# Scores of group 0 in a row, four projections moved, and two spreads that wait for rows of maxima

## The chip, the cores and the metric

The kernel runs on one core of a Trainium2 chip. The metric is the device time of one execution in microseconds (us).

## The reference, cut to what matters

Two transformer layers work on 2 batches of 512 tokens of width 256. Each has modulated layer norms, causal attention with 16 heads of 16 dims, and a mixture of experts (top 2 of 8, then top 4 of 16).

```
q, k, v = heads(h @ Wq.T), heads(h @ Wk.T), heads(h @ Wv.T)
scores  = einsum('bhqd,bhkd->bhqk', q, k) / sqrt(16)
attn    = softmax(where(causal, scores, -inf), axis=-1)
x = x + ga * (einsum('bhqk,bhkd->bhqd', attn, v) merged @ Wo.T)
x = x + gb * mixture_of_experts(layernorm(x) * (1 + cb) + sb)
```

## The kernel before, in words

All engines' programs are written out by hand in order, and meet at semaphores. `l` is the layer (0 or 1).

The projections of an attention are 12 *fills*, each one PSUM bank of 128x512: `FILLS` is q, k, q, k, v, v for batch 0 (fills 0 to 5) and v, v, q, k, q, k for batch 1 (fills 6 to 11). PE computes a fill, ScalarE (ACT) moves it out (`move_fill`, two activations for a q or k fill), and VectorE (DVE) splits q and k into three bf16 parts (`split_fill`, three operations). In layer 1 the v fills are moved by DVE inside `split_fill`, with the bias added; in layer 0 `split_fill` of a v fill does nothing.

A pair of q and k fills is a *unit*; unit u holds groups 2u and 2u+1, four heads of one batch each. `spread_unit` copies the parts of a unit into the layout that the score matmuls read: 6 DMAs of 128 KB for q and 6 for k. For units 0 and 1 SP's queue issues the q side and POOL's the k side; for units 2 and 3 POOL issues all 12. Unit 3's spread waits until the by-key scores of groups 0 and 1 are done, because it reuses unit 0's room. In layer 1 POOL issues after it one DMA of 4 MB, a part of layer 1's expert weights, and then runs five elementwise steps.

Attention goes through 8 groups (`NG`). Each is treated twice. First `scores_by_query(g, c)`, 6 pieces (`NA`): PE makes scores, DVE takes row maxima (`maxima(g, c)`) from two double banks in turn, so piece c waits for the maximum of piece c-2. `split_maxima` writes the negated maxima, PE transposes them (`turn_maxima`), DVE copies them to `mT` (`move_maxima`), and SP sends two *rows of maxima* by DMA into the q operand (`send_maxima`, 4 KB, counted in `m_rows[l][g % 2]`). Then `scores_by_key(g, c)`, 10 pieces (`NB`): PE makes scores with the maxima subtracted, ACT takes the exponent (`exponent`), and `weigh_values` and `turn_context` of the group before are worked in between, with `move_context` on ACT and `context` on DVE.

The head of an attention is the by-query scores of groups 0 and 1 mixed with fills 6 to 11. Then follows the loop over p: by-key scores of group p, by-query scores of group p+2 between them. In layer 0, DVE at the end of p = 1 also shapes the modulation rows (`modulation_rows(0)`); SP sends them to DRAM (`keep_rows`) and back over all partitions (`spread_rows`, 1 MB) before it sends the maxima of group 3. Group 3's `send_maxima` is thus queued on SP behind both.

## Time and profile before

| what | value |
|---|---|
| median of 3 runs | 643.21 us (642.0, 643.21, 648.59) |
| profiled execution, its own time | 648.09 us |
| its span from first to last instruction | 646.3 us |
| PE busy, mean granted clock | 508.9 us (79%), 0.882 of full |
| DVE busy | 362.4 us (56%) |
| ACT busy | 241.6 us (37%) |
| POOL busy | 229.3 us (35%) |
| chain that ended last | PE 61%, DVE 16%, DMA 11%, issue 5%, POOL 3%, ACT 3% |

1.8 us of the profiled execution's own time lie outside its span. That execution is 4.9 us above the median of the runs. Attention of layer 0 takes about 15 to 158 us of the span, that of layer 1 about 272 to 425; expert loops take 197 to 247 and 464 to 620.

### The profile page before, as it was taken

Reading aid. Unit: us, or ns where it says so; the run is one execution under the profiler, and the core shown is the slowest. Engines: PE = TensorE matmul, PEld = TensorE weight load, DVE = VectorE, ACT = ScalarE, POOL = GpSimd, SP = SyncE. Lnnn points to the kernel's source line nnn. Section 1 sums busy time; section 2 is a strip of 40 time slices with the busy share of each in tenths; the row PEclk is TensorE's granted clock in tenths of the full one; section 3 lists DMA queues with packets and bytes.
Section 4 is the critical chain, followed back from the end, with each engine's and each line's share of the span. In section 5 each row is a group of like instructions: output and inputs, shape, how many; then the busy total and the mean of one; then the engine's idle time right before and its main releaser. Section 6 shows DMA issues by size and latency. Waiting matters only on the chain.

```text
span 646.3 us, 9621 instructions
## 1 busy us (share of the span) xinstructions
PE 508.9 (79%) x3124; PEld 333.7 (52%) x3124; DVE 362.4 (56%) x831; ACT 241.6 (37%) x530; POOL 229.3 (35%) x233
## 2 busy tenths in 40 slices
PE   3968879997749992266889798744699999999960
PEld 3444545555437892134456365544466666666640
DVE  3529686544652341475877864489654444444425
ACT  1414556652012331030456466423344444444430
POOL 2213023001043424622301700050357777777650
PEclk9979899989567997585989999965799999999995
DMA  8587253163134432268543813460124444444446
GB/s 290 77 101 96 25 116 52 29 255 128 49 122 149 128 102 82 81 86 137 86 53 50 245 68 135 164 264 32 50 51 81 82 78 77 79 78 80 66 47 196
DMA packets 35137, 67.31 MB, mean 104 GB/s; under 512 B 6901, under 2 KB 27845, under 8 KB 34201
## 3 DMA queue, kind: packets, MB, share of 16 engines
q0 software_dynamic: 14496, 31.08, 26.9%
q1 hardware_dynamic: 20312, 35.64, 18.0%
q8 instruction: 27, 0.44, 0.3%
q14 instruction: 14, 0.11, 0.1%
q10 hardware_dynamic: 288, 0.05, 0.0%
HBM read 38.93 MB, written 14.96 MB: 83 GB/s over the span
## 4 chain that ended last, share of the span: by engine, by line
PE 61%; DVE 16%; DMA 11%; issue 5%; POOL 3%; ACT 3%; SPq 1%; POOLq 0%; DVEq 0%; ACTq 0%
PE bank L1619 15%; PE bank L1640 9%; PE bank L1484 5%; PE bank L1454 4%; PE bank L1434 4%; DVE mx L1034 4%; DMA big<-mT 3%; PE bank L1601 2%; PE bank L1372 2%; PE bank L1628 2%; PE bank L1410 2%; PE bank L1616 2%; PE bank L1587 2%; DMA wqkv<-in_wqkv_dram 2%; PE bank L1404 2%
## 5 line engine op out<-in xcount | busy, mean ns | idle before, releaser
L1034 DVE TENSOR_REDUCE mx<-bank 128x4 f32<-128x512 f32 (+2 forms) x96 | 97.9, 1041 | 41.2 <-PE bank L1437 40.7
L755 ACT ACTIVATE ptm<-bank 128x512 f32<-128x512 f32 x160 | 92.4, 597 | 60.9 <-PE bank L1457 58.0
L1619 PE MATMUL bank<-big,ptm 128*128 x280 | 111.5, 522 | 0.0
L629 POOL DMA_INDIRECT ptm<-token_rows,token x70 | 68.9, 984 | 92.8 <-DVE token L1239 47.9
L638 POOL DMA_INDIRECT sums<-ptm,token x47 | 74.4, 1583 | 30.9 <-ACT ptm L832 29.7
L431 POOL DMA_DIRECT2D big<-parts x72 | 38.8, 546 | 122.0 <-DVE parts L960 71.9
L1434 PE MATMUL bank<-big 96*128 96x128 bf16 (+3 forms) x256 | 64.4, 318 | 21.9 <-DMA big<-parts 15.2
L1454 PE MATMUL bank<-big 98*128 98x128 bf16 (+3 forms) x256 | 67.4, 308 | 11.9 <-DMA big<-mT 7.3
L1640 PE MATMUL bank<-big,ptm 128*128 (+1 forms) x280 | 72.6, 382 | 0.0
L1619 PEld LDWEIGHTS bank<-big,ptm 128*128 128x128 f32 x280 | 52.2, 201 | 25.9 <-issue 23.3
L1285 DVE TENSOR_SCALAR tok<-bank 128x256 f32<-128x256 f32 x47 | 20.0, 425 | 79.1 <-PE bank L1619 79.1
L1437 PE MATMUL bank<-constb 128*128 128x128 bf16 x256 | 52.7, 232 | 0.0
L815 ACT ACTIVATE ctxden<-tok 128x256 f32<-128x256 f32 x47 | 19.6, 417 | 86.1 <-DVE tok L1285 86.1
L1640 PEld LDWEIGHTS bank<-big,ptm 128*128 128x128 f32 (+1 forms) x280 | 48.1, 192 | 5.0
L1457 PE MATMUL bank<-constb 128*128 128x128 bf16 x256 | 48.9, 224 | 0.0
L573 POOL TENSOR_TENSOR rstd<-vareps,neghalf 128x4 f32<-128x4 f32 x8 | 8.6, 1071 | 111.0 <-DVE vareps L901 111.0
L1454 PEld LDWEIGHTS bank<-big 98*128 98x128 bf16 x256 | 25.5, 100 | 42.3 <-ACT ptm L755 17.8
L1434 PEld LDWEIGHTS bank<-big 96*128 96x128 bf16 x256 | 26.8, 105 | 38.9 <-issue 28.2
L1357 PE MATMUL bank<-consts,tok 128*128 128x128 f32 x96 | 17.3, 339 | 35.0 <-DVE tok L910 25.9
L1484 PE MATMUL bank<-ptm,big 128*32 128x128 f32 (+3 forms) x512 | 42.1, 448 | 1.4 <-ACT ptm L755 1.4
L1601 PE MATMUL bank<-consts,ptm 128*128 128x128 f32 x140 | 29.0, 291 | 11.7 <-DMA ptm<-token_rows,token 11.7
L1410 PE MATMUL bank<-feat,wqkv 128*128 128x512 f32 x64 | 34.5, 680 | 2.1 <-DMA wqkv<-in_wqkv_dram 1.1
(177 smaller groups left out, 818.9 us busy)
## 6 DMA issues: line engine op xcount, KB each, us to landing
big<-parts POOLq DMA_DIRECT2D x72, 128.0 KB, 5.8
big<-in_moe_dram SPq DMA_DIRECT2D x1, 6144.0 KB, 20.1
big<-in_moe_dram POOLq DMA_DIRECT2D x1, 4096.0 KB, 15.2
big<-in_moe_dram SPq DMA_DIRECT2D x1, 3456.0 KB, 11.2
big<-parts SPq DMA_DIRECT2D x24, 128.0 KB, 4.7
results<-ptm SPq DMA_DIRECT2D x23, 128.0 KB, 1.7
sums<-zeros SPq DMA_DIRECT2D x2, 1152.0 KB, 7.7
modbc<-modulation_rows SPq DMA_DIRECT2D x2, 1024.0 KB, 9.0
```

The lines of the kernel that those rows point to most:

```text
L629: nc.gpsimd.indirect_dma_start(out=xt[:, i % 4, :], out_offset=None, in_=xs[l][:, :], in_offset=bass.IndirectOffsetOnAxis(ap=token[:, i:i ...
L638: nc.gpsimd.indirect_dma_start(out=acc[i % 2][:, :], out_offset=bass.IndirectOffsetOnAxis(ap=token[:, i:i + 1], axis=0), in_=yt[:, i % 4, ...
L755: nc.scalar.activation(dst, src, ACT.Exp).then_inc(b_exp[l], 1)
L1034: nc.vector.tensor_reduce(mx[:, g % 2, :].rearrange("p (j i) -> p j i", j=HG)[:, j0:j0 + n, i], a_view(c), AX.X, ALU.max).then_inc(a_max[l ...
L1410: last = nc.tensor.matmul(fill_bank(n), wqkv[:, k, lo:lo + P], feat[:, k, b * S:(b + 1) * S], start=(k == 0), stop=(k == KD - 1))
L1434: nc.tensor.matmul(dst[:, j, :], qr[u][0:SROWS, hl, i * P:(i + 1) * P], kr[u][0:SROWS, hl, 0:w], start=True, stop=False)
L1437: last = nc.tensor.matmul(dst[:, j, w - P:w], ident_b, causal_b, start=False, stop=True)
L1454: nc.tensor.matmul(ps[4 + c % 2][:, col:col + S - k * P], kr[u][0:MROWS, hl, k * P:(k + 1) * P], qr[u][0:MROWS, hl, k * P:S], start=True, ...
L1457: last = nc.tensor.matmul(ps[4 + c % 2][:, col:col + P], causal_b, ident_b, start=False, stop=True)
L1484: last = nc.tensor.matmul(ps[6][32 * j:32 * j + 32, k * P:S], vaug[:, b * TB + k, hg * HG + j, :], pt[:, g % 2, j, PK[k]:PK[k] + S - k * P ...
L1619: last = nc.tensor.matmul(dst, xtT[:, off % 2, k, :], moe_w1(l, k, e), start=False, stop=(k == KD - 1))
L1640: last = nc.tensor.matmul(dst, hidT[0:HK[l], off % 2, k, :], moe_w2(l, k, e), start=False, stop=(k == 1))
```

## The change

It reorders the work at the head of both attentions and adds waits to two spreads.

- PE, layer 0: fills 6 and 7 (v, batch 1) come right after `modulation_rows(0)`, ahead of the first score. In both layers the six by-query pieces of group 0 come in a row; in layer 1 the transposition of batch 1 stays between pieces 1 and 2.
- The other fills: in layer 0 fill 8 comes after group 0's pieces and fill 9 inside group 1's; in layer 1 fills 6 to 9 come there.
- Fills 10 and 11 (unit 3) move into p = 0 of the loop, behind by-key pieces 5 and 7, into banks 6 and 7. ACT moves them out between the exponents of p = 0. PE's p = 1 begins with a wait for both moves.
- DVE: the order of `maxima` and `split_fill` follows; `split_fill(11)` goes from the end of p = 2 to the end of p = 1, where in layer 0 it stands ahead of `modulation_rows(0)`.
- Spread of unit 2 waits in addition for the rows of maxima of group 1 (`m_rows[l][1]` at 32), that of unit 3 for those of group 3 (at 64).

```
 def fill_bank(n):
-    return ps[n] if n < 4 else ps[4 + n % 2]
+    return ps[n] if n < 4 else ps[n - 4] if n >= 10 else ps[4 + n % 2]
...
+            if u == 2:
+                eng.wait_ge(m_rows[l][1], 32)
             if u == 3:
                 eng.wait_ge(b_ps[l], NB * 2)
+                eng.wait_ge(m_rows[l][1], 64)
...
-                for n in range(NFILL):
+                for n in range(10):
...
                         exponent(p, c)
+                        if p == 0 and c in (5, 7):
+                            move_fill(10 + c // 7)
...
-                maxima(0, 0)
-                maxima(0, 1)
-                split_fill(6)
-                split_fill(7)
-                for c in range(2, NA):
+                for c in range(NA):
                     maxima(0, c)
                 split_maxima(0)
+                split_fill(6)
                 move_maxima(0)
                 maxima(1, 0)
+                split_fill(7)
+                maxima(1, 1)
                 split_fill(8)
-                maxima(1, 1)
                 maxima(1, 2)
+                maxima(1, 3)
                 split_fill(9)
-                for c in range(3, NA):
-                    maxima(1, c)
+                maxima(1, 4)
+                maxima(1, 5)
                 split_maxima(1)
...
-                    if p in (0, 2):
-                        split_fill(10 + p // 2)
+                    if p < 2:
+                        split_fill(10 + p)
                     if (l, p) == (0, 1):
                         modulation_rows(0)
...
-                    elif n >= 6:
+                    elif 6 <= n < 10:
                         wait_fill_read(pe, l, n - 2)
+                    elif n >= 10:
+                        if l == 0:
+                            pe.wait_ge(rows_read, 2)
+                        pe.wait_ge(mT_ready[l], 2)
...
                     if l == 0 and n == 5:
                         modulation_rows(0)
+                        fill(6)
+                        fill(7)
...
-                            wait_fill_read(pe, l, NFILL - 2)
-                            wait_fill_read(pe, l, NFILL - 1)
+                            wait_fill_read(pe, l, 8)
+                            wait_fill_read(pe, l, 9)
...
-                fill(6)
-                scores_by_query(0, 2)
-                fill(7)
-                scores_by_query(0, 3)
-                fill(8)
-                scores_by_query(0, 4)
-                scores_by_query(0, 5)
-                fill(9)
+                for c in range(2, NA):
+                    scores_by_query(0, c)
+                fill((8, 6)[l])
                 turn_maxima(0)
+                if l == 1:
+                    fill(7)
                 scores_by_query(1, 0)
                 scores_by_query(1, 1)
-                fill(10)
+                fill((9, 8)[l])
                 scores_by_query(1, 2)
                 scores_by_query(1, 3)
-                fill(11)
+                if l == 1:
+                    fill(9)
                 scores_by_query(1, 4)
                 scores_by_query(1, 5)
                 for p in range(NG):
+                    if p == 1:
+                        wait_fill_read(pe, l, 10)
+                        wait_fill_read(pe, l, 11)
                     for c in range(NB):
                         scores_by_key(p, c)
+                        if p == 0 and c in (5, 7):
+                            fill(10 + c // 7)
```

## Rows read from the trace of the kernel before

**Rows 1.** Busy time by stage: us, PE, PEld, DVE, ACT, POOL, clock, DMA share, GB/s

```profile
32.20:37.20 5.00, 0.00 (x0) 0.00 (x0) 0.00 (x0) 1.05 (x2) 0.00 (x0) 0.88 0.65 75
37.20:42.80 5.60, 5.55 (x24) 4.47 (x25) 1.92 (x2) 0.00 (x0) 3.14 (x6) 0.50 0.81 110
...
70.30:73.50 3.20, 3.20 (x22) 2.51 (x23) 1.29 (x2) 1.19 (x2) 0.00 (x0) 0.50 0.00 0
...
294.00:305.40 11.40, 8.47 (x35) 6.37 (x36) 5.17 (x17) 1.55 (x2) 4.34 (x7) 0.50 0.92 127
```

**Rows 2.** Timeline of PE, layer 0: start, us, what, idle before it and releaser

```profile
56.03 1.93 PE L1410 MATMUL bank<-feat,wqkv 128*128 128x512 f32 x4
...
70.28 0.61 PE L1454 MATMUL bank<-big 98*128 98x512 bf16 x1 [2.52 <-DMA big<-mT]
...
86.15 0.32 PE L1434 MATMUL bank<-big 96*128 96x384 bf16 x1 [1.01 <-DVE mx L1034]
```

**Rows 3.** Timeline of DVE at the head of layer 0's attention

```profile
38.37 0.69 DVE L1034 TENSOR_REDUCE mx<-bank 128x4 f32<-128x512 f32 x1 [9.88 <-PE bank L1437]
...
56.22 0.68 DVE L958 TENSOR_TENSOR tmp<-tok,parts 128x512 f32<-128x512 f32 x1
...
58.12 3.22 DVE L1034 TENSOR_REDUCE mx<-bank 128x2 f32<-128x768 f32 x3
...
62.81 0.21 DVE L1047 COPY mT<-bank 32x128 bf16<-32x128 bf16 x1 [0.43 <-PE bank L1472]
```

**Rows 4.** The page's costliest group: busy and mean ns, idle before, releaser

```profile
L1034 DVE TENSOR_REDUCE mx<-bank 128x4 f32<-128x512 f32 (+2 forms) x96 | 97.9, 1041 | 41.2 <-PE bank L1437 40.7
```

**Rows 5.** Timeline of ACT: context copies of groups 0, 3, 4, then 0 and 3

```profile
78.46 0.60 ACT L740 ACTIVATE ctxden<-bank 128x512 f32<-128x512 f32 x1 [0.87 <-PE bank L1484]
...
111.15 0.60 ACT L740 ACTIVATE ctxden<-bank 128x512 f32<-128x512 f32 x1 [0.87 <-PE bank L1484]
...
120.83 0.60 ACT L740 ACTIVATE ctxden<-bank 128x512 f32<-128x512 f32 x1 [0.87 <-PE bank L1484]
...
341.03 0.60 ACT L740 ACTIVATE ctxden<-bank 128x512 f32<-128x512 f32 x1 [0.86 <-PE bank L1484]
...
376.12 0.60 ACT L740 ACTIVATE ctxden<-bank 128x512 f32<-128x512 f32 x1 [0.87 <-PE bank L1484]
```

**Rows 6.** Group 1's rows of maxima, layer 0: issues and time to landing

```profile
L466 SPq DMA_DIRECT2D big<-mT x2: 503/546/590, 63.0 to 63.6; - x2
...
DMA to landing us min/median/max: 6.5/6.6/6.6
```

**Rows 7.** Group 2's rows of maxima, layer 0, issued at 74.4 and 75.0

```profile
DMA to landing us min/median/max: 1.7/1.7/1.8
```

**Rows 8.** Unit 2's spread, layer 0: its last issues, at 60.5 and 61.0

```profile
DMA to landing us min/median/max: 8.3/8.4/8.4
```

**Rows 9.** Timeline of POOL: its first issue of unit 2's spread, layer 0

```profile
54.77 3.23 POOL L431 DMA_DIRECT2D big<-parts  x6 [13.97 <-DVE parts L960]
```

**Rows 10.** Unit 1's spread, layer 0: SP's last issues, at 39.9 and 40.6

```profile
DMA to landing us min/median/max: 12.6/12.7/12.8
```

**Rows 11.** The chain that ended last, around group 3's rows, layer 0

```profile
85.43 4.31 DMA modulation_rows<-big
...
90.73 4.01 DMA big<-mT
```

**Rows 12.** Timeline of PE and of DVE, layer 1, p = 4

```profile
366.14 0.23 PE L1434 MATMUL bank<-big 96*128 96x128 bf16 x1 [1.56 <-DMA big<-parts]
...
367.58 2.26 DVE L1040 SCALAR_TENSOR_TENSOR mneg<-mx,mneg 128x16 bf16<-128x16 f32 x1
```

**Rows 13.** Timeline of POOL: the 4 MB of expert weights, layer 1

```profile
360.29 0.58 POOL L586 DMA_DIRECT2D big<-in_moe_dram  x1
```

**Rows 14.** First of group 5's rows of maxima, layer 1 (issued 370.6)

```profile
DMA to landing us min/median/max: 4.7/4.7/4.7
```

**Rows 15.** Table loads of ACT at the exponent's line

```profile
L755 ACT ACT_TABLE_LOAD x2: 1283/1283/1283, 59.1 to 321.6; - x2
```

## The prediction

> **What bounds the kernel now.** I read the page's chain first: most of it is PE, with DVE and DMA for the rest. The change touches only the two attentions, so I then read their stages and each engine's timeline there. The steady part of an attention is PE without a gap: from one context copy to the next there are 9.68 us (120.83 - 111.15) [rows 5]. What can be won lies at the head and in the stalls of the first five groups.
>
> In layer 0 the head begins with PE idle for 5 us until unit 0's spread lands, and then come 5.6 us at a granted clock of 0.50 [rows 1]. Then DVE sets the pace: it works from the first maxima at 38.37 to the end of group 1's at 61.34, 23.0 us, with gaps in which PE makes fills [rows 3]. Its work alone is less: six maxima at a mean of 1.04 us are 6.2 [rows 4], twice that 12.5; two splits of 1.9 us each (58.12 - 56.22) are 3.8 [rows 3]. Next, group 1's rows of maxima take 6.6 us to land where group 2's take 1.7 [rows 6, 7]. The difference is unit 2's spread, issued from 54.77 on and landed at 69.4 (61.0 + 8.4) [rows 8, 9]; the rows land at 70.2, 0.8 later. PE waits 2.52 us for them and runs 3.2 us at half clock after it [rows 1, 2].
>
> **Part 1: the order of the head, layer 0.** Fills 6 and 7 take 1.8 us each (a fill is 1.93 us by its row, less what overlaps the next) [rows 2]. They fit into the 5 us before the first score, at no cost, and leave PE idle for only 1.5 us. Since after 2.52 us of idleness the clock was at its lower level, and after 1.01 it was not [rows 1, 2], I take it that the first scores run at the full clock, and DVE starts 0.5 us earlier, at 37.9. DVE then has six maxima (6.2), the negation (0.4) and the transposition and copy (0.7): the copy ends near 45.2. Six more maxima (6.2) and two splits (3.8) follow: 55.2, against 61.3. That is 6.1 us earlier. Group 0's rows are then issued inside unit 1's spread, which lands at 53.3 (40.6 + 12.7) [rows 10], so I expect them near 54, and by-key scores of group 0 can't start before. By-query piece (2,0), behind the first of them, waits for the fifth maximum of group 1 and so until 54 in any case; that covers it. Without this cover it costs up to 1 us.
>
> **Part 2: fills 10 and 11 in p = 0.** PE was full there, so they cost their time, 3.55 us (2 x 1.77). ACT has 10 exponents of 0.6 and gets 4 activations of 0.6: 8.4 us in a stretch of some 11, so it hides them. The wait at the head of p = 1 costs 0.2 us, the last exponent being one move behind. Both layers.
>
> **Part 3: unit 2's spread waits for group 1's rows.** These are now issued into empty queues and land in 1.7 us, at about 59.3 (56.9 for the end of the copy, 63.0 - 6.1 [rows 3], plus issues and landing). p = 0 ends at 65.2 (70.28 - 2.52 = 67.8 before [rows 2], - 6.1 + 3.55). PE's wait of 2.5 us, 2.7 with its loads, disappears, and with it 3.2 us at half clock, which cost 1.6 at most; I take 1.3, because some waits of that stretch would be there at either level. What is late next is unit 2's spread itself: 12 issues and 14.6 us from the first to the last landing (69.4 - 54.77) [rows 8, 9], so 73.9. Group 2's rows are issued inside it and land 0.8 us behind, at 74.7 (by the pattern of group 1's rows [rows 6]). Group 2's by-key scores are due at 65.2 + 9.7 = 74.9. So it just fits: 0 us, with 0 to 1 of cost.
> Sum of layer 0 up to group 2's start: 6.1 - 3.55 + 2.7 + 1.3 = 6.5 us earlier.
>
> The Trainium skill has a rule against this reading (DMA: Bandwidth & Descriptors, Queues, rings and completion order): an engine goes round its queues packet by packet, so small rows should slip in between, but a semaphore's write lands only after every earlier write of that DMA engine, across queues. By the first half alone the wait for the rows would not depend on the spread and part 3 would gain nothing; the row of 6.6 against 1.7 us sides with the second half [rows 6, 7].
>
> **Part 4: split 11 at p = 1 and unit 3's spread behind group 3's rows, layer 0.** Here the change costs. In p = 2, PE already waits 1.01 us for maxima of group 4 [rows 2]. The split (1.9 us) now stands ahead of that and of the modulation rows; PE's gap becomes 2.9 us and may lower the clock (1.6 us more). The modulation rows are ready 1.9 us later, their trip to DRAM takes 4.31 us before [rows 11]; with no spread in flight I estimate 2.1 (between 1.7, the small rows alone [rows 7], and 4.3). Group 3's rows follow behind the 1 MB copy with the same 4.0 us. So they land 13.4 us after group 2's start (13.5 before, + 1.9, - 2.2, + 0.2). Only then do the 12 DMAs of unit 3 start, and they take 14.6 us. By-query piece (6,0), in p = 4, waits for them. From group 2's start to group 5's: 13.4 + 14.6 + 9.35 for the rest of p = 4 = 37.35 us. Before it was 32.7 (111.15 - 78.46) to 32.9 [rows 5]. Cost 4.4 us; between 3 and 6.6, by the trip to DRAM. SP's queue carries group 4's rows in the same stretch, at about 12 to 13 us after the spread's start, so they come before the spread's end and do not set it.
> Layer 0: 6.5 - 4.4 = 2.1 us gained.
>
> **Part 5: layer 1.** The head runs at 0.50 clock until 305.4 [rows 1]. Six scores in a row without fills in between bring the first maxima 7 us forward, but fills 6 to 9 then all stand in group 1's part, and DVE waits for two of them. I count group 1's maxima 3.5 us earlier if the clock rises as before, 1.7 if fill 6 still runs at the lower level; I take 2.6. Then as in layer 0: - 3.55 for the fills, + 2.7 for the wait, + 1.3 for the clock. Sum 3.1 us up to group 2.
> After it: group 3's rows land 6.6 us after group 2's start (copy at 4.3 behind the split, 0.6 for the issue, 1.7 to land). Unit 3's spread lands at 21.3, group 4's rows 0.8 later, 22.1, and p = 4 would be due at 20.3. The stall is 1.8 us. POOL has issued its 4 MB behind the spread; group 5's rows end with it, about 32.3 us after group 2's start (as before, when they took 4.7 us and ended with it [rows 14]). Group 5 starts then. Before it was 35.1 (376.12 - 341.03) [rows 5], because p = 4 had two stalls: 1.56 us for the late k side of unit 3 [rows 12], and DVE held for two small operations of 2.2 us each, a tenth of which is their usual time, while POOL worked on x [rows 12]. POOL's steps now end 22.7 us after group 2's start and DVE's negation is due at 23.3, so that collision goes; with 1 us if it doesn't. Gain 2.8 us. Layer 1: 5.9 us.
> Everything later is shifted as a whole. Sum: 2.1 + 5.9 = 8.0 us of the profiled execution's 648.1, that is 640.1; taken off the median of the runs, 643.2, it gives 635.2.
>
> **The rivals.**
> A second case: the spreads are not what p = 4 waits for. A unit moves faster when only POOL's queue is at work, or p = 2 is longer for other reasons. Then layer 0 keeps 5 to 6.5 and layer 1 6 to 7: 12 us, 631. For it: no wait for unit 3 shows in layer 0 now. Against: twelve issues in a row took 14.6 us [rows 8, 9], and p = 3 lasts 9.7.
>
> A third case, slower: the 4 MB get ahead of group 4's rows, in layer 1. POOL issues them 13.1 us after group 2's start, SP the rows 13.7. Before, the weights were issued at 360.29 [rows 13], after these rows. If rows wait for all that was issued earlier, as group 5's did (landing 4.7 us, to the end of the 4 MB [rows 14]), they land 32.3 us after group 2's start instead of 22.1, which is 10.2 us more, and 1.6 for the clock after so long a gap. Sum 8.0 - 11.8 = - 3.8: 647. It decides from the point where the weights' packets stand ahead of the rows' in the rings. Against it: the weights stand behind unit 3's own spread in POOL's queue, and the rows are in another.
>
> A fourth: the head gains but all is given back, by unit 3's spread in both layers and by the clock after the gaps in p = 2 and p = 4 (1.6 us each, four times): 8.0 - 6.4 = 1.6, 641.6.
>
> A fifth: moving fills between exponents makes ACT load tables. One load is 1.28 us [rows 15]; four in p = 0 are 5.1 us, of which ACT's slack takes about half: 2.5 us in each layer, 640. No row shows Identity after Exp without a load in between, nor with one. The Trainium skill (ScalarE: Activation LUTs, Table sets: the hidden batching unit) says that identity and copy are in every set, by which there is none; the copies of context between exponents load nothing, which agrees for copy.
>
> **How the numbers follow.** Chances: the forecast 0.44 (632 to 639), the second 0.18, the third 0.12, the fourth 0.18, the fifth 0.08. About 1%, 6.4 us, is what a measurement here can tell from no change: below 636.8 is faster, above 649.6 slower. Of the forecast I put two thirds below 636.8, and all of the second: 0.29 + 0.18 = 0.47, with 0.02 of the fourth, where only one gap lowers the clock, 0.49. Slower: 0.05 of the third and some for what I have not seen, 0.08. The rest, 0.43, is within 1%. Range: from the second case, with 1 us for its bounds, 630, to the third, 646.5.
>
> **What would show it.** Right: no PE gap before fills 6 and 7, clock at 1.00 at the first scores; mT of group 0 near 45; group 1's rows landing in about 2 us and no wait for them; a wait for big<-parts at p = 4 of layer 0, of 2 to 4 us; group 4's rows in layer 1 landing in about 7 us. Wrong: 0.50 clock at the first scores (part 1), table loads in p = 0 (fifth), rows of maxima that land in 15 us (third), or no wait at p = 4 (second). The prediction fails as a whole if the head's gain doesn't reach group 2, or if unit 3's spread costs more than 8 us over both layers.

## The result, and the profile after

The changed kernel takes 651.15 us at the median of 20 runs (646.74 to 654.48); the kernel before, run beside it on the same chip, takes 647.42. The ratio is 1.0068, with an interval of 1.0048 to 1.0088: slower by 0.7%, some 4.4 us, where 8.0 us of gain was forecast. It lies inside the 1% taken for no change and above the predicted range. The forecast's 635.2 was taken off a median of three runs, 643.2; over 20 runs the kernel before stands at 647.42, so 4.2 us of the distance from 635.2 to 651.15 are the base and not the change. Executions in a slower state (one of before at 1759.65 us here; 653.28 and 2102.96 of before and 735.08 of e9 later) count in the medians but not in the ratios. The profiled execution took 646.74 us, the quickest of its 20 (span 644.9), so the changed kernel was run and traced once more (e8 below); what both traces show is taken as the change's work.

The timeline of ACT shows where the time went. Copies of context, group 0 and group 3 of layer 0, then the same of layer 1; the rows of before are [rows 5].

```profile
73.69 0.60 ACT L743 ACTIVATE ctxden<-bank 128x512 f32<-128x512 f32 x1 [0.86 <-PE bank L1494]
...
111.16 0.60 ACT L743 ACTIVATE ctxden<-bank 128x512 f32<-128x512 f32 x1 [0.86 <-PE bank L1494]
...
335.95 0.60 ACT L743 ACTIVATE ctxden<-bank 128x512 f32<-128x512 f32 x1 [0.86 <-PE bank L1494]
...
374.59 0.60 ACT L743 ACTIVATE ctxden<-bank 128x512 f32<-128x512 f32 x1 [0.86 <-PE bank L1494]
```

In layer 0 the first copy comes 4.8 us earlier (78.46 to 73.69), and at group 3's all of it has been given back (111.15, 111.16). In layer 1 the copies 0 and 3 were 35.09 us apart and are 38.64 apart now; the prediction had 32.3. The cause stands in the timeline of PE. Its idle spells of more than a microsecond, layer 0 and then layer 1 (start, us, what, idle before and releaser); of before [rows 2, 12]:

```profile
49.75 0.38 PE L1444 MATMUL bank<-big 96*128 96x512 bf16 x1 [1.52 <-DVE mx L1039]
53.08 0.61 PE L1464 MATMUL bank<-big 98*128 98x512 bf16 x1 [1.76 <-DMA big<-mT]
...
83.23 0.48 PE L1444 MATMUL bank<-big 96*128 96x384 bf16 x1 [2.87 <-DVE mx L1039]
...
104.48 0.39 PE L1464 MATMUL bank<-big 98*128 98x512 bf16 x1 [2.49 <-DMA big<-mT]
...
311.50 0.38 PE L1444 MATMUL bank<-big 96*128 96x512 bf16 x1 [1.69 <-DVE mx L1039]
315.41 0.26 PE L1444 MATMUL bank<-big 96*128 96x128 bf16 x1 [2.06 <-DVE mx L1039]
...
366.42 0.61 PE L1464 MATMUL bank<-big 98*128 98x512 bf16 x1 [6.64 <-DMA big<-mT]
```

The last row is the third case: PE stands 6.64 us for group 4's rows of maxima. Why they are late is seen on POOL, whose issues and steps in the same stretch are these (before, the weights went at 360.29 [rows 13]):

```profile
346.40 6.27 POOL L434 DMA_DIRECT2D big<-parts  x12 [17.85 <-DMA big<-mT]
352.66 0.58 POOL L589 DMA_DIRECT2D big<-in_moe_dram  x1
353.26 1.27 POOL L595 TENSOR_TENSOR wqkv<-wo,modbc 128x512 f32<-128x512 f32 x1
```

and on SP's queue, which sends group 4's rows 0.2 us after the weights:

```profile
352.86 1.14 SPq L469 DMA_DIRECT2D big<-mT  x2
```

The two land 12.0 us later at the median; before, the same two rows were issued 2.6 us ahead of the weights and landed in 4.2. The DMA view of 352.8 to 354, issues with KB and time to landing:

```profile
big<-mT SPq DMA_DIRECT2D x2, 4.0 KB, 12.0
```

What the DMA engines did in between: packets, MB and share by queue (q0 is POOL's, q1 SP's), from 353.5 to 360:

```profile
q0 software_dynamic: 273, 1.16, 117.2%
q8 instruction: 1, 0.02, 1.7%
```

and from 360 to 366.4:

```profile
q0 software_dynamic: 77, 2.40, 89.0%
q1 hardware_dynamic: 64, 0.01, 0.9%
```

None of the rows' 64 packets moves before 360, while unit 3's spread drains; then they move among the packets of the 4 MB. In the last stretch q0's are 31 KB each (2.40 MB over 77).

The stages of [rows 1] without the third, and four others: us, PE, PEld, DVE, ACT, POOL, granted clock, DMA share, GB/s.

```profile
32.20:37.20 5.00, 5.00 (x24) 3.35 (x23) 0.00 (x0) 1.85 (x4) 0.00 (x0) 1.00 0.59 69
37.20:42.80 5.60, 4.36 (x32) 2.38 (x30) 5.14 (x6) 0.41 (x1) 3.13 (x6) 1.00 0.88 119
53.00:66.60 13.60, 12.99 (x74) 7.62 (x75) 7.86 (x11) 7.39 (x14) 6.04 (x12) 0.78 0.38 56
...
83.20:88.00 4.80, 4.77 (x30) 2.37 (x34) 3.00 (x4) 1.19 (x2) 0.00 (x0) 0.50 0.53 219
...
294.00:305.40 11.40, 10.15 (x58) 7.55 (x59) 8.28 (x15) 1.55 (x2) 2.36 (x5) 0.83 1.07 178
359.80:366.40 6.60, 0.00 (x0) 0.00 (x0) 2.57 (x3) 0.60 (x1) 2.40 (x2) 0.73 0.87 365
366.40:370.00 3.60, 3.58 (x24) 2.68 (x24) 0.69 (x1) 1.19 (x2) 0.00 (x0) 0.55 0.85 364
```

PE is full ahead of the first scores, and they run at 1.00 where they ran at 0.50. But behind the two gaps at 49.75 and 53.08 the clock is at its lower level for part of the stretch, 0.78 from 53.0 to 66.6; before it was 1.00 there. Finer stretches show that it is the lower level from 53 to 59, with PE full:

```profile
53.00:55.00 2.00, 1.92 (x14) 1.33 (x15) 1.93 (x5) 0.60 (x1) 0.00 (x0) 0.50 0.00 0
...
57.00:59.00 2.00, 2.00 (x13) 1.27 (x12) 1.36 (x3) 1.19 (x2) 0.00 (x0) 0.50 0.01 2
59.00:61.00 2.00, 2.00 (x13) 1.25 (x12) 1.82 (x2) 1.19 (x2) 0.44 (x1) 0.99 0.01 2
```

After the 2.87 us at p = 2 of layer 0 the clock is 0.50, after the 6.64 us 0.55.

DVE at the head of layer 0: the six maxima of group 0, and the copies of group 0's and group 1's transposed maxima [rows 3]:

```profile
37.65 5.95 DVE L1039 TENSOR_REDUCE mx<-bank 128x4 f32<-128x512 f32 x6 [7.93 <-PE bank L1447]
...
44.34 0.21 DVE L1052 COPY mT<-bank 32x128 bf16<-32x128 bf16 x1 [0.32 <-PE bank L1482]
...
57.37 0.21 DVE L1052 COPY mT<-bank 32x128 bf16<-32x128 bf16 x1 [1.71 <-PE bank L1482]
```

Group 0's rows, issued at 44.6 and 45.2, land in 8.0 us, with unit 1's spread; group 1's, issued at 57.6 and 58.2 into empty queues, in 1.7 (DMA view of 57 to 59; before 6.6 [rows 6]):

```profile
big<-mT SPq DMA_DIRECT2D x2, 4.0 KB, 1.7
```

### The profile page after: what moved, and what is told of

Its sections match the earlier page's. It is cut to its first block, busy times and chain, and to the rows that moved or that the text cites. A ratio compares the mean times of both kernels' runs of the same rounds, so it can differ in the third digit from the quotient of the medians.

```text
span 644.9 us, 9625 instructions
## 1 busy us (share of the span) xinstructions
PE 506.8 (79%) x3124; PEld 331.9 (51%) x3124; DVE 359.5 (56%) x831; ACT 241.4 (37%) x530; POOL 229.1 (36%) x233
## 4 chain that ended last, share of the span: by engine, by line
PE 65%; DVE 15%; DMA 9%; issue 5%; ACT 3%; POOL 2%; SPq 1%; DVEq 0%; POOLq 0%; ACTq 0%
PE bank L1632 15%; PE bank L1653 9%; PE bank L1464 5%; PE bank L1494 5%; DMA big<-mT 5%; PE bank L1444 4%; PE bank L1418 4%; DVE mx L1039 3%; PE bank L1614 3%; PE bank L1641 2%; PE bank L1376 2%; PE bank L1629 2%; PE bank L1600 2%; PE bank L1361 2%; PE bank L1447 2%
## 5 line engine op out<-in xcount | busy, mean ns | idle before, releaser
L758 ACT ACTIVATE ptm<-bank 128x512 f32<-128x512 f32 x160 | 92.5, 597 | 69.2 <-PE bank L1467 66.2
L1632 PE MATMUL bank<-big,ptm 128*128 x280 | 109.9, 516 | 0.0
L641 POOL DMA_INDIRECT sums<-ptm,token x47 | 74.4, 1583 | 31.2 <-ACT ptm L837 29.6
L1464 PE MATMUL bank<-big 98*128 98x128 bf16 (+3 forms) x256 | 69.6, 315 | 16.8 <-DMA big<-mT 10.9
L1444 PE MATMUL bank<-big 96*128 96x128 bf16 (+3 forms) x256 | 66.1, 324 | 20.0 <-DVE mx L1039 11.1
L1447 PE MATMUL bank<-constb 128*128 128x128 bf16 x256 | 53.4, 235 | 0.6 <-issue 0.6
L1467 PE MATMUL bank<-constb 128*128 128x128 bf16 x256 | 50.0, 228 | 0.0
```

Source lines behind the costliest of these rows:

```text
L641: nc.gpsimd.indirect_dma_start(out=acc[i % 2][:, :], out_offset=bass.IndirectOffsetOnAxis(ap=token[:, i:i + 1], axis=0), in_=yt[:, i % 4, ...
L758: nc.scalar.activation(dst, src, ACT.Exp).then_inc(b_exp[l], 1)
L1444: nc.tensor.matmul(dst[:, j, :], qr[u][0:SROWS, hl, i * P:(i + 1) * P], kr[u][0:SROWS, hl, 0:w], start=True, stop=False)
L1447: last = nc.tensor.matmul(dst[:, j, w - P:w], ident_b, causal_b, start=False, stop=True)
L1464: nc.tensor.matmul(ps[4 + c % 2][:, col:col + S - k * P], kr[u][0:MROWS, hl, k * P:(k + 1) * P], qr[u][0:MROWS, hl, k * P:S], start=True, ...
L1467: last = nc.tensor.matmul(ps[4 + c % 2][:, col:col + P], causal_b, ident_b, start=False, stop=True)
```

## The experiments

All kernels were traced and timed beside the kernel before. The segment between the two attentions, which no edit touches (copy 7 of layer 0 to the first score of layer 1), took 141.8 to 145.3 us from trace to trace, so whole times of single traces vary by some us. I compare stages within an attention, from the timelines of ACT and PE, and whole kernels by the ratio. All in us; "to copy 0" of layer 1 counts from its first score, "to copy 7" too.

Stages vary as well where the code is the same. Copy 0 of layer 0 comes at 78.46 and 76.06 with the head of before (before, e11) and at 73.35 to 76.48 with the changed one (changed, e8, e1, e5, e2, e3); copies 0 to 3 of layer 0 take 36.8 to 39.8 in the four traces with all of layer 0 as changed (changed, e8, e1, e5); layer 1 to copy 0 takes 45.2 to 46.6 and 43.6 to 45.3. From copy 5 to copy 6, where the edits change nothing, it is 13.2 us or 14.8 to 14.9; the longer form has 3 us at 0.50 to 0.52 clock behind the same 0.96 us of idleness, and it stands in layer 0 of before, e7, e12 and e6 and in layer 1 of e6. Only copies 0 to 7 of layer 1 are steady: 75.5 and 75.9 in the two traces of the changed kernel, 76.0 in e3, and 71.9, 71.9 and 72.2 in before, e7 and e11. So differences of 2 or 3 us in layer 0 or ahead of copy 0 of layer 1, from one trace each, show little; those from copy 0 to 7 of layer 1 show much. The traces of changed, e2, e4, e9, e10 and e11 are each the quickest execution of their kernel.

| kernel | l0: copy 0 at | copies 0 to 3 | copy 5 at | l1: to copy 0 | copies 0 to 3 | to copy 7 | ratio (95%) |
|---|---|---|---|---|---|---|---|
| before | 78.46 | 32.69 | 129.49 | 46.63 | 35.09 | 118.52 | 1 |
| changed | 73.69 | 37.47 | 129.50 | 45.05 | 38.64 | 120.50 | 1.0068 (1.0048 to 1.0088) |
| e8 changed again | 76.48 | 36.77 | 131.59 | 45.34 | 39.03 | 121.19 | 1.0056 (1.0028 to 1.0084) |
| e1 | 73.35 | 37.18 | 128.87 | 44.02 | 33.39 | 114.22 | 0.9996 (0.9956 to 1.0035) |
| e5 | 73.98 | 39.75 | 132.08 | 43.61 | 31.99 | 117.20 | 1.0048 (1.0013 to 1.0083) |
| e2 | 73.70 | 38.72 | 130.76 | 43.93 | 35.91 | 116.65 | 1.0027 (0.9993 to 1.0061) |
| e3 | 75.18 | 36.70 | 130.22 | 44.00 | 39.22 | 120.04 | 1.0009 (0.9970 to 1.0048) |
| e12 | 76.03 | 38.69 | 133.06 | 44.26 | 39.18 | 120.25 | 1.0056 (1.0026 to 1.0087) |
| e4 | 75.79 | 34.86 | 129.00 | 42.79 | 37.36 | 116.96 | 0.9985 (0.9947 to 1.0024) |
| e6 | 69.21 | 39.19 | 126.75 | 41.90 | 40.82 | 121.19 | 1.0007 (0.9979 to 1.0035) |
| e7 | 76.90 | 34.05 | 129.29 | 46.14 | 35.07 | 118.02 | 1.0006 (0.9976 to 1.0036) |
| e9 | 70.39 | 36.92 | 125.65 | 41.91 | 34.62 | 113.34 | 0.9915 (0.9885 to 0.9945) |
| e10 | 70.96 | 36.62 | 128.28 | 41.65 | 34.87 | 113.34 | 0.9879 (0.9847 to 0.9910) |
| e11 | 76.06 | 30.80 | 127.68 | 45.23 | 35.39 | 117.44 | 0.9976 (0.9954 to 0.9999) |

**e1: the 4 MB behind POOL's steps and after group 7's rows have landed.** From the changed kernel:

```
-                if l == 1:
-                    nc.gpsimd.dma_start(big[:, 0:UNIT_AT[2]], ...)
...
                     ins.then_inc(bo_added, 1)
+                    pool.wait_ge(m_rows[1][1], 128)
+                    nc.gpsimd.dma_start(big[:, 0:UNIT_AT[2]], ...)
```

> The changed kernel, with the 4 MB of layer 1's expert weights moved on POOL's queue from behind unit 3's spread to behind the rows of maxima of group 7. Theory A (the weights in flight hold group 4's rows of maxima): PE's gap of 6.64 us at the start of p = 4 in layer 1 shrinks to 1 to 2 us, group 4's rows land in 7 to 8 us instead of 13, the half clock after the gap goes, and the kernel is 6 to 7 us faster than the changed one, near 645 on a median of before of 647.4. Theory B (unit 3's own spread holds the rows): the gap stays above 5 us and the time is that of the changed kernel. Nothing else should move; the experts of layer 1 start some 70 us later, so the late load costs nothing.

Measured 646.85 us, ratio 0.9996. The gap at p = 4 of layer 1 falls from 6.64 us to this:

```profile
361.54 0.61 PE L1464 MATMUL bank<-big 98*128 98x512 bf16 x1 [1.91 <-DMA big<-mT]
```

The attention of layer 1 takes 114.2 us instead of 120.5 and 121.2. The part of it that the edit can reach, copies 0 to 7, takes 70.2 instead of 75.5 and 75.9. That is the third case shown: the 4 MB ahead of the rows cost 5.3 to 5.7 us. The row also gives the forecast its due: without the weights the stall was to be 1.8, and it is 1.91. But 5.3 us come back after the attention (238.8 us from the last copy to the end, against 233.5), where the expectation had the late load free. The weights, issued at 386.98, are now in flight with a 48 KB load that DVE needs, issued at 386.42:

```profile
400.92 0.55 DVE L980 CAST parts<-parts 16x768 bf16<-16x768 f32 x1 [10.00 <-DMA parts<-in_bias_dram]
```

In the changed kernel the same wait is 2.80 us. By these stages e1 should be no faster than changed as a whole, but its ratio lies some 4 us lower; the rest comes from stages that the edit doesn't reach and stays open.

**e5: the 4 MB as soon as group 4's rows have landed.**

```
                 if l == 1:
+                    pool.wait_ge(m_rows[1][0], 96)
                     nc.gpsimd.dma_start(big[:, 0:UNIT_AT[2]], ...)
```

> The changed kernel with the 4 MB of expert weights held back on POOL's queue until group 4's rows of maxima have landed, and in no other place. Theory A (what is issued ahead of a small transfer holds it): group 4's rows land 0.8 us behind unit 3's spread as in the run with the late weights, PE's gap at the head of p = 4 in layer 1 is about 2 us instead of 6.64; group 5's rows now meet the weights and may cost 1 to 3 us at p = 5; the load of the biases, late in the run with the late weights, is on time again, and from the last context copy of layer 1 to the end there are 233 us, not 239. Together 3 to 5 us faster than the changed kernel. Rival: the span behind the attention is long for another reason, and stays at 239 us or changes without the weights.

Measured 649.08, ratio 1.0048. POOL issues the weights at 363.26, and the stall moves one group on: p = 4 waits 1.77 us, p = 5 waits 3.30.

```profile
363.03 0.39 PE L1465 MATMUL bank<-big 98*128 98x512 bf16 x1 [1.77 <-DMA big<-mT]
...
375.89 0.60 PE L1465 MATMUL bank<-big 98*128 98x512 bf16 x1 [3.30 <-DMA big<-mT]
```

From copy 0 to 7 of layer 1 it is 73.6 us, 1.9 to 2.3 better than changed and 3.4 worse than e1; the end doesn't suffer (234.2). The ratio can't tell it from changed, where 3 to 5 us were expected. So the place of this one DMA decides: ahead of group 4's rows it costs 5.3 to 5.7 us, ahead of group 5's 3.4, beside the 48 KB load 5.3.

**e2: unit 3's spread without its wait for group 3's rows.**

```
             if u == 3:
                 eng.wait_ge(b_ps[l], NB * 2)
-                eng.wait_ge(m_rows[l][1], 64)
```

> The changed kernel without the wait of unit 3's spread for group 3's rows. Theory A: in layer 0 p = 4 loses its gap of 2 to 3 us, but the modulation rows and group 3's rows travel beside the spread again, so p = 3 starts later by 0 to 2 us; in layer 1 the weights are issued 3 to 4 us earlier than in the changed kernel and still stand ahead of group 4's rows, so the gap at p = 4 stays at 3 us or more. Together 2 to 5 us faster than the changed kernel. If the wait itself were the cause of the loss in layer 1, the gap at p = 4 of layer 1 would vanish and the kernel would be 8 to 10 us faster.

Measured 648.69, ratio 1.0027. Layer 0 gains nothing (copies 0 to 3: 38.72 against 37.47 and 36.77): PE's wait moves from group 4's rows, 2.49 us in the changed kernel, to group 3's, 2.32. In layer 1 PE waits 2.59 us for group 3's rows and 1.60 for group 4's (3 or more were expected), and copies 0 to 7 take 72.7 us. So this wait is neutral in layer 0 and harmful in layer 1, by 2.7 to 3.1 us; there it sends the weights, which stand behind the spread, from 10.3 us ahead of group 4's rows (347.36, 357.65) to 0.2 us ahead of them.

**e12: unit 2's spread without its wait for group 1's rows.**

```
-            if u == 2:
-                eng.wait_ge(m_rows[l][1], 32)
```

> The changed kernel without the wait of unit 2's spread for group 1's rows. Theory A (the wait is what makes group 1's rows land in 1.7 us): they land in 6 us or more, with fills 10 and 11 in p = 0 PE then waits about 1 to 2 us for them at the head of p = 1, while group 2's rows land in 1.7 instead of 4.8 us; 0 to 2 us slower than the changed kernel. Rival (p = 0 has grown long enough for the rows to land in any case): the same time, and the wait is worth nothing.

Measured 651.5, ratio 1.0056, the same as changed. The rows, issued at 60.3 and 60.9, land in 6.8 us again (DMA view):

```profile
big<-mT SPq DMA_DIRECT2D x2, 4.0 KB, 6.8
```

and yet PE has no gap of a microsecond before group 1: with two fills more in p = 0, group 1's scores are due later than the late rows. That is the expectation's rival. PE's gap, which Part 3 credited with 2.7 + 1.3 us, goes by the fills as well as by the wait; the wait wins it only where p = 0 is short.

**e4: the two waits alone, in the kernel before.**

```
+            if u == 2:
+                eng.wait_ge(m_rows[l][1], 32)
             if u == 3:
                 eng.wait_ge(b_ps[l], NB * 2)
+                eng.wait_ge(m_rows[l][1], 64)
```

> The kernel before with nothing but the two new waits of the spreads. Theory A: group 1's rows land in 1.7 instead of 6.6 us in both layers, PE's gaps of 2.52 and 2.67 us and the half clock behind them go (3.8 us each); in layer 0 unit 3's spread begins with group 3's rows and ends p = 4 about 4 us late; in layer 1 nothing changes there, since the k side waits for its split in any case and the weights stay behind group 4's rows. Sum 3 us faster than before, 644. Rival (the rows are slow for another reason than the spread): gaps as before, and slower than before by the 4 us in layer 0, 651.

Measured 646.01, ratio 0.9985. Here the first wait is worth 2.7 us in layer 0 (the first score at 37.24, before 37.25, at 0.50 clock in both) and 2.4 to 3.8 in layer 1 (to copy 0, against e11 and before), and no gap is left before group 1. But from copy 0 to 3 it takes 2.2 and 2.3 us more, and the first thing met there is the same wait's own price, PE idle for group 2's rows behind unit 2's later spread (layer 0; 2.54 us in layer 1):

```profile
81.16 0.61 PE L1457 MATMUL bank<-big 98*128 98x512 bf16 x1 [2.49 <-DMA big<-mT]
```

The sum, 2.1 us, is less than the timing can tell.

**e3: split 11 behind the modulation rows.**

```
-                    if p < 2:
+                    if p < 2 and (l, p) != (0, 1):
                         split_fill(10 + p)
                     if (l, p) == (0, 1):
                         modulation_rows(0)
+                        split_fill(11)
```

> The changed kernel with split 11 behind the shaping of the modulation rows in layer 0 instead of ahead of it. Theory A (group 3's rows, hung behind the modulation rows, start unit 3's spread, and that ends p = 4): rows shaped 1.9 us earlier, unit 3's spread starts 1.5 to 2 us earlier and the context copy of group 3 comes 1 to 2 us earlier; the kernel is 1 to 2 us faster than the changed one. Rival (p = 2's gap of PE, from maxima of group 4 behind all of DVE's work, sets it): nothing moves, because that work is the same.

Measured 649.66, ratio 1.0009. Unit 3's spread starts 15.0 us after copy 0, against 15.9 to 17.2 in the four traces with layer 0 as changed, and PE waits 1.69 us at p = 4 instead of 2.4 to 3.1. Copies 0 to 3 take 36.70 us in layer 0, against 36.8 to 39.8: some 1 us as far as the gap tells, less than the scatter of the stage. PE's 2.87 us at p = 2 are still there, since the maxima of group 4 come behind both. Layer 1, where nothing was changed, is as slow as changed (gap 6.91). The ratio lies lower than its stages explain; I take it for scatter and leave it open.

**e6: fills 10 and 11 back in the head**, with their banks and waits of before; the order of group 0's scores and the waits of the spreads kept.

```
                 scores_by_query(1, 3)
-                if l == 1:
-                    fill(9)
+                fill((10, 9)[l])
                 scores_by_query(1, 4)
+                fill((11, 10)[l])
                 scores_by_query(1, 5)
+                if l == 1:
+                    fill(11)
...
-                        if p == 0 and c in (5, 7):
-                            fill(10 + c // 7)
```

> The changed kernel with fills 10 and 11 back in the head, between the scores of group 1 and in the banks of before; all else as changed. Theory A (in p = 0 PE is full and each fill costs its 1.8 us, while in the head PE waits for maxima, 1.52 and 1.76 us in layer 0 and 1.69 and 2.06 in layer 1, and falls to half clock): the first context copy comes 3 to 4 us earlier in each layer and the clock of p = 0 is 1.00 instead of 0.78; that is kept to the end of both attentions, since unit 3's spread hangs on group 3's rows; 6 us faster than the changed kernel. Rival (the head is full too): first context copy within 1 us of the changed kernel's.

Measured 647.06, ratio 1.0007. The first copy comes at 69.21, 4.5 us before the changed kernel's, and 3.1 earlier in layer 1. The three traces with this head (e6, e9, e10) have it at 69.2 to 71.0, the six with the changed one at 73.4 to 76.5; in layer 1 it is 41.7 to 41.9 against 43.6 to 45.3. The stage 53.0 to 66.6 at 1.00 clock, where it was 0.78:

```profile
53.00:66.60 13.60, 11.89 (x112) 7.29 (x110) 12.38 (x19) 10.29 (x19) 6.38 (x12) 1.00 0.43 64
```

PE has 112 entries there instead of 74. So the two fills in p = 0, with the gaps and the clock that they leave in the head, cost at least 2.4 us in layer 0 and 1.7 in layer 1; 3.55 each was forecast, without the clock. But PE now waits for group 2's rows (2.85 and 2.17 us), as in e4, layer 1's gap for group 4's rows stays (7.01), and to copy 7 nothing is won there (1.6 us of it by the longer form of copies 5 to 6). As a whole it is 3 to 4 us faster than changed by the ratios; 6 were expected.

**e7: fills 6 and 7 of layer 0 ahead of the first score, alone, in the kernel before.**

```
                     if l == 0 and n == 5:
                         modulation_rows(0)
+                        fill(6)
+                        fill(7)
```

> The kernel before with nothing but fills 6 and 7 of layer 0 moved ahead of the first score. Theory A (part 1 of the prediction): PE's gap of 5.1 us becomes about 1.3, the first scores run at the full clock, and DVE reaches group 1's last maxima about 3 us earlier, since pieces 2 and 3 of group 0 no longer wait behind a fill at half clock (3.66 and 1.94 us); group 1's rows still take 6.6 us. First context copy of layer 0 near 75.5 instead of 78.5; 3 us faster than before. Rival (DVE's work sets the head whatever PE does): first context copy within 1 us of 78.5.

Measured 646.1, ratio 1.0006. PE's idle time before the first score falls from 5.10 to 1.26 us and the clock behind it is 0.69 from 37.2 to 42.8, not 1.00; copy 0 gains 1.6 us, and the gap before group 1 grows to 3.33 (rows still held by unit 2's spread). To copy 5 it is 0.2. 3 us were expected; the 1.6 are no more than e11's trace has with the head of before.

**e8: the changed kernel once more.**

> The changed kernel once more, for its spread between executions and a second trace. If its loss lies in the attentions as in the first trace, the gap before group 4's by-key scores in layer 1 is again 5 us or more, and the attentions together last 2 us longer than before. If the first trace was a lucky one (its time is the lowest of its 20 runs), this one shows more or longer stretches at half clock there, and a median of the granted clock below that of before. The ratio to before is expected at 1.005 to 1.009.

Measured 650.32, ratio 1.0056. Against the trace of before: layer 0 + 2.1 us to copy 5 and + 0.5 to copy 7 (before has the longer form of copies 5 to 6), layer 1 + 2.7. The stages thus give 3.2 to 4.8 us, the ratios of the changed kernel 3.6 and 4.4. In this trace 1.28 us of idleness stand before the first score, and the head doesn't get the full clock:

```profile
37.20:42.80 5.60, 4.24 (x29) 2.27 (x30) 3.93 (x5) 0.00 (x0) 3.14 (x6) 0.78 0.72 102
```

**e9: e6, with the 4 MB once group 5's rows have landed, behind POOL's steps.**

```
                     ins.then_inc(bo_added, 1)
+                    pool.wait_ge(m_rows[1][1], 96)
+                    nc.gpsimd.dma_start(big[:, 0:UNIT_AT[2]], ...)
```

> The changed kernel with fills 10 and 11 back in the head, and the 4 MB of weights of layer 1 issued once group 5's rows of maxima have landed (behind POOL's elementwise steps). Theory A (weights ahead of rows, and rows ahead of by-key scores): group 4's rows cost PE about 2 us instead of 7, group 5's none, group 6's 0 to 1, and the biases come in time: from the first score of layer 1 to the last context copy 114 to 115 us (changed kernel 120.5 and 121.2), from there to the end 233. In layer 0 the context copies as in the run with the fills in the head (69.2, 108.4). Together 7 to 9 us faster than the changed kernel, ratio to before 0.990 to 0.994. Rival (a later wait takes its place): ratio 0.998 or more.

Measured 642.77, ratio 0.9915. POOL issues the weights in time for the end and after the rows:

```profile
364.40 0.62 POOL L612 DMA_DIRECT2D big<-in_moe_dram  x1 [5.42 <-DMA big<-mT]
```

PE has no wait over 0.3 us for rows in p = 4 or p = 5 of layer 1, and the end takes 233.3 us:

```profile
359.20 0.39 PE L1458 MATMUL bank<-big 98*128 98x512 bf16 x1 [0.29 <-DMA big<-mT]
```

e9 differs from e6 by the place of the 4 MB alone. The ratios, 1.0007 and 0.9915, are 5.9 us apart and their intervals don't touch; copies 0 to 7 of layer 1 take 71.4 us against 79.3, which is 7.9, or 6.2 without the longer form of copies 5 to 6. This is the clearest price of that one DMA. Both stages gain against before: 3.8 us in layer 0 and 5.2 in layer 1. That is 9.0 of stages against 5.5 of the ratio; the trace is of the quickest execution. PE still waits for group 2's rows, 2.46 and 2.98 us.

**e10 and e11: the modulation rows at p = 4 instead of p = 1**, SP's two copies after group 5's rows; in e9 and in the kernel before.

```
-                    if l == 0 and g == 2:
+                    if l == 0 and g == 5:
                         keep_rows(0)
...
-                    if (l, p) == (0, 1):
+                    if (l, p) == (0, 4):
                         modulation_rows(0)
```

> The kernel of the run before this one, with the shaping of layer 0's modulation rows moved from the end of p = 1 to the end of p = 4, and their trip to DRAM and back behind group 5's rows instead of group 2's. Theory A (in layer 0 group 3's rows, and so unit 3's spread, hang on the modulation rows): from the context copy of group 0 to that of group 1 it is 11 us instead of 15, unit 3's spread starts 6 us earlier and p = 4 is no longer held; the attention of layer 0 ends 5 us earlier, ratio to before 0.982 to 0.988. Rival (POOL waits for the modulation rows before it gates the output weights, or group 6's rows are held by the 1 MB instead): the gain is under 2 us.

> The kernel before with nothing but the same move of the modulation rows. Theory A: p = 2 and p = 3 of layer 0 take 9.7 to 10.7 us instead of 11.3 and 11.7; 2 to 3 us faster than before, ratio 0.995 to 0.997. If the rows of group 3 are not what holds p = 3 (split 11 and the spread are), ratio 0.999 to 1.001.

Measured 639.47, ratio 0.9879, and 645.31, ratio 0.9976. In the kernel before, copies 0 to 3 of layer 0 take 1.9 us less, since PE's gaps at p = 2 (1.01) and before group 3 are gone; the latter was this:

```profile
94.79 0.39 PE L1454 MATMUL bank<-big 98*128 98x512 bf16 x1 [2.11 <-DMA big<-mT]
```

But copies 3 to 5 then take 20.8 us instead of 18.3, so that copies 0 to 5 take 51.6 us against 51.0 in before (52.4 in e7): the modulation rows at p = 4 take it back, and that the ratio's 0.2% come from here isn't shown. e10 is the fastest kernel of the case, 1.2% below before. What it has over e9 stays open: the intervals (0.9847 to 0.9910, 0.9885 to 0.9945) overlap, and in its one trace copy 5 comes at 128.28, later than e9's 125.65, with PE waiting for maxima and for group 5's rows; its whole trace is 1.4 us shorter all the same, by 3.4 us between the attentions, where nothing was changed:

```profile
115.22 0.32 PE L1438 MATMUL bank<-big 96*128 96x384 bf16 x1 [0.96 <-DVE mx L1037]
122.54 0.39 PE L1458 MATMUL bank<-big 98*128 98x512 bf16 x1 [0.79 <-DMA big<-mT]
```

## Why the prediction was wrong

The change slowed the kernel by 0.7% where a gain was forecast. By stages, forecast against measured (changed, e8), in us, minus for earlier:

| stage | forecast | measured |
|---|---|---|
| layer 0 to copy 0 | - 6.5 | - 4.8, - 2.0 |
| layer 0, copies 0 to 3 | + 4.4 | + 4.8, + 4.1 |
| layer 1 to copy 0 | - 3.1 | - 1.6, - 1.3 |
| layer 1, copies 0 to 3 | - 2.8 | + 3.6, + 3.9 |
| sum | - 8.0 | + 2.0, + 4.7 |

**Part 5 failed, at "group 4's rows 0.8 later, 22.1".** The figure took the rows' landing from unit 3's spread and left the 4 MB, issued 0.2 us ahead of them on another queue, out of the sum. Layer 1 from copy 0 to 3 missed by 6.4 to 6.7 us of the 12.4 by which the forecast missed; e1 gives 5.3 to 5.6 of them to the 4 MB, and 1.1 stay open. The third rival had the order right, weights 0.6 us ahead of the rows (0.2 in the trace). It stood there at 0.12, with "the rows are in another" queue against it. e1, e5 and e9 show that the other queue is no protection. The rival's size was too high: it put the landing at the end of the 4 MB; those landed at 371.3 and the rows at 366.4, after the spread and among packets of the weights, and the gap was 6.64 where it had some 12. 8.0 less 5.3 to 5.6 us would have left some 2.5 of gain; what took them is the next point. With both points mended (e9) the kernel is 0.9% faster than before, 5.5 us of the 8.0.

**Part 1 failed second: it gave the clock behind the head's new gaps no price.** The gaps themselves were foreseen. PE waits 1.52 us for a maximum and 1.76 us for group 0's rows, which land at 53.0 (near 54 was forecast). By-query piece (2,0) had to wait for the fifth maximum of group 1, as written; that was done at 53.5 and the piece ran at 53.65, so the cover held. But behind these gaps PE ran at half clock from 53 to 59, where it was full: up to 3 us, with no term in the sum, in which the head fell short by 1.7 us (4.5 in e8). The price of Part 2, 3.55 us in each layer because "PE was full there", left the same thing out: e6, with one gap of 0.97 us at 54.16, has 1.00 clock there, and its first copy is 4.5 and 3.1 us earlier than the changed kernel's, 2.4 to 7.3 and 1.7 to 3.7 over all traces. A lesser miss: `turn_maxima(1)` stands in PE's order behind the first three by-key pieces, and the copy of the transposed maxima begins at 57.37 instead of 56.7, which costs nothing here.

**Part 1's clock was half right.** "I take it that the first scores run at the full clock": they did in the first trace, in which PE had no idle time there; in e8, with 1.28 us, they didn't. From 40.4 to 46.0 it was 0.50 in e8 and 1.00 in the first trace; that can be most of the 2.8 us between the two at copy 0.

**Part 3: right mechanism, no value here.** The rows land in 1.7 us and no gap is left. But e12 shows that p = 0, longer by the two fills, hid the rows anyway. So the 4.0 us belong in the sum, beside the 3.55 of the fills, and were put down to the wrong cause: the wait adds nothing. In the kernel before, without the longer p = 0, it earns 2.7 us in layer 0 and 2.4 to 3.8 in layer 1 (e4). What is late next was named rightly, group 2's rows inside unit 2's spread. They cost nothing in the changed kernel, as forecast, but 2.2 to 3.0 us wherever p = 0 is shorter (e4, e6, e9, e10).

**Part 4: right in size, in part by luck**, 4.4 against 4.8 and 4.1 (4.1 to 7.1 over the four traces with this layer 0). The gap of 2.9 us at p = 2 is there (2.87), with the lower clock that was left as a "may". At p = 4 PE waits 2.49 us, and for group 4's rows, not for the spread's parts: "they come before the spread's end" was wrong, they were issued at 95.1 and took 8.8 us, to the spread's end. The same "other queue" error as in Part 5, without the 4 MB to make it dear. Without the wait for group 3's rows as much is lost to those (e2), and split 11 has some 1 us (e3). The trip to DRAM was 1.4 us, not 2.1.

**The other rivals.** The second (spreads not binding) fell: e1, without the weights, leaves 1.91 us at p = 4. The fourth was right on the lower clock behind the gaps at p = 2 of layer 0 (0.50) and p = 4 of layer 1 (0.55); it left out the gaps and the clock in the head. The fifth fell: ACT's only table loads in the attentions are the two at the exponent's line [rows 15], now at 48.5 and 311.1, ahead of p = 0, so Identity between exponents loads nothing.

## What to carry to other kernels

When a wait or a reordering moves a big DMA, list every small transfer that is issued within a few us of it on any queue, and ask which now comes second: two 4 KB transfers took 8.3 us behind a spread (e1) and 12.0 behind a spread and 4 MB here. Placing the 4 MB later cost as much again where it met the next load that an engine waits for (e1). Before a piece of PE work is moved out of a stage, ask whether PE waits in that stage, since there the piece can be free and its absence may cost clock as well. Where a wait removed and a stage made longer close the same gap, credit it once, and test which of the two did it (e12, e4).

## What the runs showed of the hardware

- Rows of maxima of 4 KB on SP's queue moved not one packet in 6.5 us in which POOL's queue had 273. The Trainium skill (DMA: Bandwidth & Descriptors, Queues, rings and completion order) says that each engine goes round its queues packet by packet, a packet being typically 9 to 17 descriptors and at most 64. That small rows would then slip in between, as the prediction put it, is not what this trace shows. Whether the rule itself is at fault stays open: 273 of the profile's packets are 17 for each of the 16 engines, and no run tells how many of them make one packet of the skill's. Behind the 4 MB alone the rows' first packets also moved only some 4 us after the issue (e2: issued at 357.65, first packet after 361.5; e5: 365.67 and 369.5). Nor is it only the semaphore's order that delays, which the prediction took from the same section: the data themselves started late.
- The same two 4 KB transfers landed in 1.7 us with empty queues, 4.2 to 8.8 behind spreads of 128 KB pieces, 4.7 to 8.7 behind the 4 MB alone ([rows 14], e9, e2, e5), 12.0 to 12.3 behind spread and 4 MB (changed, e8, e3, e12, e6).
- What the clock did after PE's idle spell before the first score, as granted from 37.2 to 42.8: 0.48 us (e1, e2), 0.57 (e5), 0.67 (e9) and 1.12 us (e6) left it at 1.00; 1.14 us (e3) gave 0.64, 1.25 (e10, e12) 0.69 and 0.74, 1.26 (e7) 0.69, 1.28 (e8) 0.78, 3.87 (e11) 0.70, and 4.69 (e4) and 5.10 (before) 0.50. Elsewhere it is no clearer: e9 stood 2.32 us ahead of its first by-key score (at 55.34), with PE full from 49 to 53, and ran at 1.00 on both sides, where the changed kernel, after spells of 1.52 and 1.76 us, ran at 0.50. So the length of a spell alone doesn't tell the clock, and an edit that shortens one to just over a microsecond is no sure gain.
